# The front of a one-core Mamba and expert kernel written anew: table sets, softplus corrections, tap products and dummy products

## The reference

```python
xs = _clamp(_ln_c(x)).reshape(B, C, L).transpose(0, 2, 1)                 # norm per token over 128 channels
xs = _clamp(_layernorm(xs, norm_w, norm_b))
xin, z = jnp.split(xs @ in_proj_w.T, 2, axis=-1)                          # 256 inner channels each
xc = silu(conv(xin, conv_w) + conv_b)                                     # depthwise, 4 causal taps
xdbl = xc @ x_proj_w.T;  dt, Bm, Cm = split(xdbl)                         # 8, 16, 16 columns
dt = jax.nn.softplus(dt @ dt_proj_w.T + dt_proj_b)
def step(h, inp):                                                         # over 256 positions
    dA = jnp.exp(dt_t[..., None] * A)
    h = dA * h + (dt_t * x_t)[..., None] * B_t[:, None, :]
    y = jnp.einsum('bdn,bn->bd', h, C_t)
```

## Time and profile before

| | us |
|---|---|
| median of 3 runs | 208.72 |
| lowest, highest | 206.53, 208.76 |
| profiled execution | 208.26 |
| its span, first to last instruction | 206.5 |
| busy in the span: TensorE, VectorE | 183.0, 130.9 |
| busy in the span: ScalarE, GpSimd | 122.5, 105.3 |

### The profile page before, as it was taken

How to read it: one execution, slowest core, us unless ns; L and a number is a source line. 1 busy time by engine, 2 the same in 40 slices (tenths; PEclk the granted TensorE clock), 3 DMA queues, 4 the chain that set the end, 5 groups by cost and what they waited for, 6 DMA issues and landing times. The chain is left out here.

```text
span 206.5 us, 3725 instructions
## 1 busy us (share of the span) xinstructions
PE 183.0 (89%) x1202; PEld 151.8 (73%) x1202; DVE 130.9 (63%) x312; ACT 122.5 (59%) x281; POOL 105.3 (51%) x140
## 2 busy tenths in 40 slices
PE   6899868996797389799998999999998999999993
PEld 5677744652262134478997989899998999999992
DVE  2575999999999869951373836562357573334333
ACT  2707998999543564424567646776555555455540
POOL 5510044779787795692555435544375344444400
PEclk9999999999999769999999999999999999999999
DMA  5950299997560000000000000000000000000000
GB/s 154 327 176 0 71 363 349 326 317 212 184 227 0 0 0 0 0 0 3 0 2 0 3 2 0 3 0 0 3 0 5 0 2 0 3 27 3 0 0 25
DMA packets 7233, 14.38 MB, mean 70 GB/s; under 512 B 512, under 2 KB 3112, under 8 KB 6960
## 3 DMA queue, kind: packets, MB, share of 16 engines
q1 hardware_dynamic: 7216, 14.17, 21.3%
HBM read 13.88 MB, written 0.29 MB: 69 GB/s over the span
## 5 line engine op out<-in xcount | busy, mean ns | idle before, releaser
L345 POOL TENSOR_TENSOR hc<-hs,cb 128x1024 f32<-128x1024 f32 x16 | 37.6, 2355 | 25.0 <-DMA cb<-c_rows 13.0
L905 DVE SCALAR_TENSOR_TENSOR acc<-dbx_ps,comb,acc 128x128 f32<-128x128 f32 x96 | 29.0, 345 | 33.4 <-PE dbx_ps L1184 33.0
L1156 PE MATMUL bc_ps<-x_hi,w_hi 128*128 128x256 f32 x128 | 42.3, 330 | 0.8 <-DVE dbx_ps L761 0.8
L612 ACT ACTIVATE hid<-bc_ps,par 128x256 f32<-128x256 f32 x64 | 26.8, 471 | 25.3 <-PE bc_ps L1158 25.1
L359 POOL TENSOR_TENSOR w_lo<-w1b,w_hi 128x256 fp32r<-128x256 f32 x32 | 23.5, 736 | 27.4 <-ACT w_hi L604 27.1
L771 DVE TENSOR_TENSOR_SCAN hs<-da,dbx_ps 128x1024 f32<-128x1024 f32 x16 | 36.4, 2278 | 0.1
L1158 PE MATMUL bc_ps<-x_hi,w_lo 128*128 128x256 f32 x128 | 36.0, 281 | 0.0
L1157 PE MATMUL bc_ps<-x_lo,w_hi 128*128 128x256 f32 x128 | 35.8, 280 | 0.0
L1184 PE MATMUL dbx_ps<-w2b,hid 128*128 128x128 f32 (+1 forms) x256 | 33.9, 276 | 0.8 <-DVE acc L905 0.8
L1184 PE MATMUL dbx_ps<-w2a,hid 128*128 128x128 f32 x256 | 34.1, 276 | 0.3 <-ACT hid L612 0.2
L359 POOL TENSOR_TENSOR w_lo<-w1a,w_hi 128x256 fp32r<-128x256 f32 x32 | 23.2, 732 | 21.6 <-ACT w_hi L604 21.6
(11 more groups left out here) (178 smaller groups left out, 233.7 us busy)
## 6 DMA issues: line engine op xcount, KB each, us to landing
w1a<-w_in SPq DMA_DIRECT2D x2, 1024.0 KB, 8.9
cb<-c_rows SPq DMA_DIRECT2D x2, 1024.0 KB, 6.1
w1b<-w_in SPq DMA_DIRECT2D x2, 1024.0 KB, 14.4
cb<-c_rows SPq DMA_DIRECT2D x2, 768.0 KB, 5.6
cb<-taps_in SPq DMA_DIRECT2D x1, 512.0 KB, 4.9
cb<-c_rows SPq DMA_DIRECT2D x2, 256.0 KB, 3.7
par<-packed_in SPq DMA_DIRECT2D x1, 473.0 KB, 3.8
x_cm<-x_in SPq DMA_DIRECT2D x2, 128.0 KB, 2.1
```

The lines of the kernel that those rows point to most:

```text
L345: nc.gpsimd.tensor_tensor(hc[p][:], hs[p][:], cb[:, k].rearrange("p i (o t) -> p i o t", o=1).to_broadcast([128, PAIR, DC, T]), ALU.mult). ...
L612: ins = nc.scalar.activation(hid[p][:, c, :], h_ps[p][:, T * c:T * (c + 1)], ACT.Gelu, bias=par[:, bass.ds(u * UC + at, 1)])
L905: nc.vector.scalar_tensor_tensor(acc[k][:, t, :], o_ps[:, w // span % RING, 128 * t:128 * (t + 1)], comb[layer][b][:, t, bass.ds(u, 1)], a ...
L1156: nc.tensor.matmul(h_ps[p][:, T * c:T * (c + 1)], w1_hi[w][:, at], x_hi[b][:], start=True, stop=False)
```

## The change

- `natural_log_exp_and_others` takes the place of `exp_and_others` from the first convolution's SiLU on, and the loads of `natural_log` and back fall away, two for each batch. At the start `exp_and_others` stays.
- With that set, ScalarE takes the logarithm of 1 once, in one column `ln_one`, between the two halves of batch 0's softplus. It is subtracted wherever a logarithm goes into `dt`.
- Batch 0's correction e - ((1 + e) - 1) is made by GpSimd (`low_parts`), and VectorE adds it; VectorE's five passes a half become four, in another order. The copies of C rows and B columns go from VectorE to ScalarE, between and behind the two logarithms.
- `taps_in` goes: VectorE reads the tap rows from SBUF. The first half's taps are made in two parts of two taps, with the norm's step between; TensorE waits for the second part inside the convolution.
- ScalarE's `x_tok` copy of batch 0 is ahead of `w_dt` now, and the diagonals (`skip_rows`) behind it.
- `wide` sends dummy products of 256 columns without a wait in front; they replace all but one of the narrow ones.

```diff
-        plan = [("constants",), ("x_stats", 0), ("x_stats", 1), ("rows_out",), ("taps_in", 0), ("x_norm", 0), ("taps_in", 1),
-                ("inner_x", 0), ("taps", 0), ("in_proj", 0), ("taps", 1), ("x_norm", 1), ("conv", 0), ("conv", 1), ("v", 0),
+        plan = [("constants",), ("x_stats", 0), ("x_stats", 1), ("x_norm", 0), ("rows_out",),
+                ("inner_x", 0), ("taps", 0, 0), ("in_proj", 0), ("taps", 0, 1), ("taps", 1), ("x_norm", 1), ("conv", 0), ("conv", 1), ("v", 0),
...
+            def low_parts():
+
+                for c in range(DC):
+                    low, e = dt_a[0][:, c], dt_e[0][:, c]
+                    pool.wait_ge(s["one_e"], c + 1)
+                    nc.gpsimd.tensor_tensor(low, e, low, ALU.subtract).then_inc(s["low_done"], 1)
...
+                elif (step, *arg) == ("softplus", 0):
+                    low_parts()
...
                 if c == DC - 1:
-                    nc.scalar.preload_act_table_set("exp_and_others")
+                    nc.scalar.preload_act_table_set("natural_log_exp_and_others")
...
-                    nc.scalar.preload_act_table_set("natural_log")
+                        if c == 0:
+                            act.wait_ge(s["ones_ready"], 1)
+                            nc.scalar.activation(ln_one[:], ones[:, 0:1], ACT.Ln).then_inc(s["ln_one_ready"], 1)
                     for c in range(DC):
                         act.wait_ge(s["exp_dt"], c + 1)
                         nc.scalar.activation(dt_l[0][:, c], dt_e[0][:, c], ACT.Ln, bias=ones[:, 0:1]).then_inc(s["ln_dt"], 1)
-                    nc.scalar.preload_act_table_set("exp_and_others")
+                        if c == 0:
+                            act.wait_ge(s["bct_ps"], 1)
+                            nc.scalar.activation(c_row[:, 0, :], bct_ps[0][0:NS, T:2 * T], ACT.Copy).then_inc(s["c_row_ready"], 1)
...
-            def taps(c):
+            def taps(c, half=None):
...
-                dve.wait_ge(s["taps_ps"], c + 1)
+                dve.wait_ge(s["taps_loaded"], 16)
+                at = slice(0, TAPS) if half is None else slice(TAPS // 2 * half, TAPS // 2 * (half + 1))
...
+                def with_log(c):
+                    dve.wait_ge(s["ln_dt"], c + 1)
...
+                    link(nc.vector.scalar_tensor_tensor(dt_q[0][:, c], dt_l[0][:, c], ln_one[:, 0:1], dt_q[0][:, c],
+                                                        ALU.subtract, ALU.add))
+
+                def with_low(c):
+                    dve.wait_ge(s["low_done"], c + 1)
+                    nc.vector.tensor_tensor(dt[:, c, 0, :], dt_q[0][:, c], dt_a[0][:, c], ALU.add).then_inc(s["dt0_ready"], 1)
...
+            def wide(n):
+
+                for _ in range(n):
+                    nc.tensor.matmul(warm_ps[:, 0:T], ident[:], ones[:], start=True, stop=True)
+
             def x_stats(b):
                 if b == 0:
-                    keep_warm("ident_ready", 1)
+                    keep_warm("ident_ready", 1, 1)
+                    pe.wait_ge(s["ones_ready"], 1)
+                    wide(1)
...
+                if b:
+                    wide(4)
...
-                for sem, value, n in (("wv_ps", 1, 3), ("var2", 1, 2), ("rstd2", 1, 1)):
-                    keep_warm(sem, value, n)
+                wide(2)
...
                 if b == 0:
-                    keep_warm("xs_tok", 1, 2)
+                    wide(2)
...
+                    if (b, c, k) == (0, 0, TAPS // 2):
+                        pe.wait_ge(s["taps_ready"], 2)
```

More of the change, by code:

```diff
@@ L631, in experts @@
                         high_part(k + 1, u + STAGED - UNITS, u % STAGED)
-            does = {"constants": constants, "rows_out": rows_out, "taps_in": taps_in, "x_norm": x_norm, "conv": conv, "softplus": softplus,
+            does = {"constants": constants, "rows_out": rows_out, "x_norm": x_norm, "conv": conv, "softplus": softplus,
                     "bc_copy": bc_copy, "silu1": silu1, "stage": stage,
@@ L686, in x_stats @@
                 batch_statistics(b, x_at[b], "var1")
[L688 removed]
+            def taps(c, half=None):
                 dve.wait_ge(s["params_loaded"], 16)
[L691 removed]
+                dve.wait_ge(s["taps_loaded"], 16)
+                at = slice(0, TAPS) if half is None else slice(TAPS // 2 * half, TAPS // 2 * (half + 1))
                 w_in = col("in_w")[:, 128 * c:128 * (c + 1)].rearrange("p (o d) -> p o d", o=1)
[L693 to L694 removed]
+                nc.vector.tensor_tensor(w_tap[:, c, at], w_in.to_broadcast([C, at.stop - at.start, 128]),
+                                        taps_sb[:, c, :].rearrange("p (k d) -> p k d", k=TAPS)[:, at], ALU.mult).then_inc(s["taps_ready"], 1)
             def x_norm(b):
@@ L725, in softplus @@
                     return
+                def with_log(c):
+                    dve.wait_ge(s["ln_dt"], c + 1)
+                    if c == 0:
+                        dve.wait_ge(s["ln_one_ready"], 1)
+                    dve.wait_ge(s["r_done"], c + 1)
+                    link(nc.vector.scalar_tensor_tensor(dt_q[0][:, c], dt_l[0][:, c], ln_one[:, 0:1], dt_q[0][:, c],
[3 more added lines that the diff above has]
+                    nc.vector.tensor_tensor(dt[:, c, 0, :], dt_q[0][:, c], dt_a[0][:, c], ALU.add).then_inc(s["dt0_ready"], 1)
                 for c in range(DC):
-                    g, low, e = dt_q[0][:, c], dt_a[0][:, c], dt_e[0][:, c]
                     dve.wait_ge(s["abs_done"], c + 1)
-                    nc.vector.tensor_scalar(g, dt0_ps[c][:, 0:T], col("dt_b")[:, c:c + 1], 0.0, ALU.add, ALU.max).then_inc(s["r_done"], 1)
+                    nc.vector.tensor_scalar(dt_q[0][:, c], dt0_ps[c][:, 0:T], col("dt_b")[:, c:c + 1], 0.0, ALU.add,
+                                            ALU.max).then_inc(s["r_done"], 1)
                     dve.wait_ge(s["exp_dt"], c + 1)
-                    dve.wait_ge(s["r_done"], c + 1)
-                    nc.vector.tensor_tensor(g, g, e, ALU.add)
-                    link(nc.vector.tensor_scalar(low, e, 1.0, 1.0, ALU.add, ALU.subtract))
-                    link(nc.vector.tensor_tensor(g, g, low, ALU.subtract))
-                    if c == 0:
-                        bc_copy()
+                    nc.vector.tensor_scalar(dt_a[0][:, c], dt_e[0][:, c], 1.0, 1.0, ALU.add, ALU.subtract).then_inc(s["one_e"], 1)
                 for c in range(DC):
-                    dve.wait_ge(s["ln_dt"], c + 1)
-                    nc.vector.tensor_tensor(dt[:, c, 0, :], dt_q[0][:, c], dt_l[0][:, c], ALU.add).then_inc(s["dt0_ready"], 1)
+                    with_log(c)
+                    with_low(c)
                 dve.wait_ge(s["dt0_ready"], DC)
@@ L751, in rounding @@
                 link(nc.vector.tensor_scalar(halves(f_ps), dt_e[1][:], 1.0, 1.0, ALU.add, ALU.subtract))
-                nc.vector.tensor_tensor(dt_q[1][:], halves(f_ps), dt_e[1][:], ALU.subtract).then_inc(s["rounded"], 1)
+                nc.vector.scalar_tensor_tensor(dt_q[1][:], halves(f_ps), ln_one[:, 0:1], dt_e[1][:],
+                                               ALU.add, ALU.subtract).then_inc(s["rounded"], 1)
             def inputs(b, k, p):
```

26 lines of the change are left out of this document (10 added, 16 removed).

## The result

| us | before | after |
|---|---|---|
| median of 6 runs | 208.66 | 205.66 |
| lowest, highest | 206.53, 208.78 | 205.48, 206.12 |
| profiled execution | 208.26 | 206.1 |
| its span | 206.5 | 204.3 |

The ratio of the times is 0.9879, with a 95% interval of 0.984 to 0.9919: 1.2% faster. That is less than 2%, but the interval excludes no change.

What follows compares the result with a forecast made beforehand. The start of the recurrence's first VectorE product, behind a four-engine chain, was taken to bound what the change could gain. Savings of 2.01 + 0.57 - 0.06 = 2.5 us from 208.26 gave 205.8 us, range 203.7 to 207.7.

Steps and rivals of the forecast that it cites:

- The convolution: TensorE's front: with the clock up by 8 us, it starts near 11.1 and takes 3.62 us instead of 5.20.
- dummies in the queue when `xs_b` is ready: Sign of a wrong forecast: TensorE still has dummy products queued when VectorE's `xs_b` ends, at 9.69.
- `Abs`: ScalarE's first softplus step in batch 0: moves from 18.88 to 16.87, 2.0 us earlier, waiting for TensorE.
- the transposes of batch 1 end last: TensorE's queue ahead of the second step-size product: they wait for batch 1's `xs_b` at 15.91, limiting the gain to 2.0 us.
- Softplus: From `Abs` to the recurrence's first product: 5.37 us instead of 5.94, 0.57 saved, with GpSimd contention delaying VectorE's first add.
- The rival without contention: VectorE and GpSimd do not disturb each other in softplus: first product at 21.7, time 205.2; chance 0.08.
- C rows: Copy ready 2.1 us earlier while VectorE moves 2.6; GpSimd's first weighing thus moves 0.5 less, absorbed by ring buffers.
- The clock drop: Rival: the 0.50 granted-clock stretch moves past 80 us into the experts, losing 3.4 us: 209.2; chance 0.05.
- from there every row of the recurrence 2.5 us earlier: Sign of a right forecast: after the first product near 22.2, all recurrence rows shift by 2.5 us.
- the sum: Whole kernel: 2.01 + 0.57 - 0.06 = 2.5 us off the profiled 208.26, giving 205.8.
- The second level of times: Rival: before's one run 2.2 us under the others has a later cause that remains, giving 204.0; chance 0.22.

Runs made afterwards that it cites:

- the PSUM run: The changed kernel with `dt_q` of batch 0 in a PSUM bank, so VectorE's adds have one SBUF input: 205.18 us, ratio 0.9867 against the kernel before.

## Why the prediction was right

The forecast was 205.8; the median is 205.66.

- **The convolution.** Forecast: start about 11.1, clock up by 8, 3.62 us. Measured: 11.15, up at 7.32, 3.72. `xs_b` started at 8.96, as worked out. The dummies were out of the way only just in time: forecast free at 9.3, they ended at 9.78 by the trace's modelled ends, and `xs_b` at 9.69. So one of the forecast's own signs of being wrong, dummies in the queue when `xs_b` is ready, stood at its edge. It cost nothing: the transposes started at 9.74, forecast 9.75.
- **`Abs`.** Forecast 16.87, measured 16.88, and it waits for TensorE with the load long over. The reading that the transposes of batch 1 end last, and not the convolution, holds: `xs_b` of batch 1 ended at 15.91 (15.18 + 0.73), and the transposes started at 15.97.
- **Softplus.** Forecast: the first add drawn out to 20.22 by GpSimd, L777 at 22.24. Measured: it ends at 20.19, the correction add starts at 20.22, L777 at 22.26. That there is contention was read rightly from the earlier trace rows, and the PSUM run confirms it, with 0.55 us. Its size was luck in part: the row has VectorE end 0.03 behind GpSimd, and the 0.3 of the forecast came from no row; measured it was 0.29. The rival without contention would have had 21.7, and that run, with one SBUF input, had it (21.71).
- **C rows.** "It moves 0.5 less than VectorE" failed. GpSimd's first weighing moved from 28.44 to 25.89, by 2.55, and is put down to the scan, no longer to the load. Nothing hung on it.
- **The clock drop.** The rival had 0.05 for a drop that moves into the experts and costs 3.4 us. A small form of it happened: the low stretch grew from 6.75 to 10.1 us, and the router's products fell into it. The step that failed is "from there every row of the recurrence 2.5 us earlier" taken through to the end: 2.56 arrived at the first product, 2.17 at the router. By the profiled executions alone the gain is 2.16 us, not 2.5, and after's took 206.1, not the 205.8 of the sum. The forecast also let the recurrence end at 80 us; before's last scans ran from 85.01 to 89.47, beside the first expert products. In five of the other profiles a drop did reach past 80 us, by up to 2.2 us.
- **The median.** It moved by 3.0 us, more than the profiled pair. The profiled execution of before was faster than five of its six timed runs (208.26 against a median of 208.66), and that of after slower than four of its other five (206.1 against 205.66). So that the forecast is met within 0.2 is in part two deviations that cancel.
- **The second level of times.** The forecast gave 0.22 to a level that stays in the changed kernel. No run of after came near 204.0. The kernel before ran anywhere from 206.3 to 209.3 in these comparisons, after with narrow products from 205.75 to 208.30, after with wide ones nearly always within 0.7 us, and after without any from 207.17 to 208.84. That the spread belongs to the moment at which the clock rises in the front is argued, not shown: the rise was at 14.89 in before's profile and at 14.21 in that with one table set, but none of their runs near 206.5 has a profile. Against it as the only cause, before with wide dummies had four of ten runs at 208.64 or above, and after with two table sets, its wide dummies in place, ran from 206.97 to 209.12.
- **No single part carries it.** The forecast counted 2.0 us for what precedes `Abs` and 0.57 for what follows. The wide products alone gave the first, by 1.88 us, in the one execution profiled. The second needs the changed order on VectorE and the one table set together: the set alone had a ratio of 1.0004, the order with two sets 1.0006.

What sets when the clock falls in the recurrence, and for how long (3.4 to 10.2 us in these profiles), stays open. It fell in different places in kernels that are alike there, and no run shows its rule.

## What to carry to other kernels

Find the queue that ends last before a load or a pass is removed: the table load was worth nothing until VectorE's order was changed, and 1.26 us at the first scan afterwards. What a pass moved to GpSimd saves is lost again if VectorE's next instruction reads two SBUF inputs at that time; one input in PSUM avoids it. Dummy products that fill TensorE's queue early were worth 2.7 us here against none, as much as the whole change gained. Those in the recurrence brought nothing. A drop of the clock costs by where it falls: read that in the changed profile, in more than one execution, with what ends last there.
